# Three late expert weights loaded early, inputs turned two tiles ahead, and a GpSimd product by a broadcast tensor in an attention and mixture-of-experts block

## What is computed

```
mod = (silu(c) @ wmod) in 6 parts: sa, ca, ga, sb, cb, gb        # |ga|, |gb| at least 0.25, sign kept
h = layernorm(x) * (1 + ca) + sa
x = x + ga * attention(h)       # 16 heads of 16, causal softmax, output projection
h = layernorm(x) * (1 + cb) + sb
logits = h @ gate_w             # 8 experts, the 2 largest taken, softmax over the two
y = sum over the two of weight_e * (silu(h @ w1[e]) @ w2[e])     # 256 -> 512 -> 256
x = x + gb * y
```

## Time and profile before

| | |
|---|---|
| median of 3 runs | 1025.18 us (1021.88 to 1030.54) |
| the profiled execution | 1022.33 us, its span 1020.6 us |
| TensorE matmul / VectorE / ScalarE / GpSimd busy | 89% / 71% / 57% / 36% |
| chain that ended last, by engine | PE 60%, DVE 14%, ACT 9%, issue 6%, DMA 4%, POOL 3% |
| Silu of a tile (L1050) | 598 ns mean, 71 of them |
| high part of a tile's inputs (L1044), low part (L1451) | 378 and 424 ns median |
| low part of a tile's hidden values (L1456) | 690 ns mean |
| GpSimd's product with a broadcast tensor (L906) | 747 to 1027 ns, median 750, 9 of them |
| GpSimd's division (L865) | 2361 ns mean |

### The profile page before, as it was taken

How to read it: one execution, slowest core, us unless ns; L and a number is a source line. 1 busy time by engine, 2 the same in 40 slices (tenths; PEclk the granted TensorE clock), 3 DMA queues, 4 the chain that set the end, 5 groups by cost and what they waited for, 6 DMA issues and landing times.

```text
span 1020.6 us, 19387 instructions
## 1 busy us (share of the span) xinstructions
PE 904.9 (89%) x6174; PEld 532.1 (52%) x6174; DVE 727.4 (71%) x2328; ACT 577.6 (57%) x1257; POOL 371.9 (36%) x320
## 2 busy tenths in 40 slices
PE   6899799998899999989999888778799999999990
PEld 3543335433535334544443443322698898999880
DVE  8788766879576889657789677877447574444687
ACT  3345576676576677586676657757434443334452
POOL 1422030251423124324103333074386466565530
PEclk7999999999999999999999999999899999999995
DMA  8456526426406257254365473104423213222789
GB/s 276 125 63 126 76 68 137 76 64 118 71 9 139 56 86 144 76 60 112 53 117 116 110 146 138 35 25 127 136 75 97 94 64 109 74 80 72 219 271 299
DMA packets 83236, 110.62 MB, mean 108 GB/s; under 512 B 15930, under 2 KB 56434, under 8 KB 83138
## 3 DMA queue, kind: packets, MB, share of 16 engines
q1 hardware_dynamic: 75506, 89.45, 38.7%
q0 software_dynamic: 6816, 18.62, 5.8%
q10 hardware_dynamic: 816, 1.32, 0.4%
HBM read 69.42 MB, written 35.41 MB: 103 GB/s over the span
## 4 chain that ended last, share of the span: by engine, by line
PE 60%; DVE 14%; ACT 9%; issue 6%; DMA 4%; POOL 3%; SPq 2%; another core or an unknown queue 1%; POOLq 0%; ACTq 0%; DVEq 0%
PE PO L1612 10%; PE PH L1489 8%; PE PY L1489 8%; PE PS L1592 8%; PE PM L1569 7%; ACT PR L992 3%; PE PHT L1697 2%; PE PX L1624 2%; PE PX L1538 2%; DVE MXF L1295 2%; DVE JK L1292 2%; DMA LD<-OS 2%; PE PS L1596 2%; PE PX L1547 1%; PE PX L1548 1%
## 5 line engine op out<-in xcount | busy, mean ns | idle before, releaser
L992 ACT ACTIVATE PR<-PS 128x512 f32<-128x512 f32 (+3 forms) x768 | 334.5, 497 | 149.9 <-PE PS L1596 113.3
L1292 DVE CUSTOM_DVE_ANT_0 JK<-PM,MK 128x128 bf16<-128x128 f32 (+3 forms) x512 | 239.1, 484 | 54.7 <-PE PM L1569 53.5
L1569 PE MATMUL PM<-QK 128*128 128x512 bf16 (+3 forms) x768 | 247.4, 331 | 24.7 <-DVE MXF L1295 15.2
L1592 PE MATMUL PS<-QK 128*128 128x512 bf16 (+3 forms) x768 | 245.9, 331 | 12.6 <-ACT PR L992 10.4
L1295 DVE TENSOR_REDUCE MXF<-PM 128x1 f32<-128x512 f32 x256 | 175.2, 685 | 76.8 <-PE PM L1569 75.0
L1592 PEld LDWEIGHTS PS<-QK 128*128 128x128 bf16 x768 | 74.9, 98 | 170.3 <-ACT PR L992 105.0
L1612 PE MATMUL PO<-PR,V 128*17 128x512 f32 (+3 forms) x1536 | 162.8, 496 | 0.0
L1569 PEld LDWEIGHTS PM<-QK 128*128 128x128 bf16 x768 | 75.1, 98 | 100.4 <-DVE MXF L1295 37.4
L1489 PE MATMUL PY<-W2S,HT 128*128 x852 | 120.4, 291 | 5.5 <-issue 5.3
L1489 PE MATMUL PH<-W1S,XT 128*128 x426 | 114.0, 403 | 7.9 <-DVE XT L1451 6.9
L1050 ACT ACTIVATE HS<-PH 128x512 f32<-128x512 f32 x71 | 42.5, 598 | 138.4 <-PE PH L1489 115.6
(11 more groups left out here) (263 smaller groups left out, 1210.0 us busy)
## 6 DMA issues: line engine op xcount, KB each, us to landing
QK<-SD SPq DMA_DIRECT2D x180, 128.0 KB
SD<-SP SPq DMA_DIRECT2D x42, 256.0 KB, 2.8
OP<-OS SPq DMA_DIRECT2D x64, 64.0 KB
LP<-LR SPq DMA_DIRECT2D x64, 64.0 KB, 2.3
W1S<-in_w SPq DMA_DIRECT2D x8, 512.0 KB, 7.2
W2S<-in_w SPq DMA_DIRECT2D x8, 512.0 KB, 4.6
X<-XA SPq DMA_DIRECT2D x3, 1024.0 KB, 9.6
H2D<-XA SPq DMA_DIRECT2D x3, 1024.0 KB, 4.9
```

Of the source, the lines that this page charges most:

```text
L992: eng.activation(PR[:, slot, i, c0:512], PS[m % 3][:, c0:512], ACT.Exp, scale=0.25).then_inc(S["exp"].sem, 1)
L1292: eng.tensor_tensor_reduce(JK[:, jk % 2, 0:w], PM[m % 3][:, 0:w], MK[:, 512 - w:512], 1.0, -3.0e38, ALU.add, ALU.max, MXA[:, mb, h, qt:qt ...
L1569: eng.matmul(PM[m % 3][:, 0:128 * (k1 - k0)], QK[:, r, h, 0, qt * 128:(qt + 1) * 128], QK[:, r, h, 1, k0 * 128:k1 * 128], start=True, stop ...
L1592: last = eng.matmul(PS[m % 3][:, c0:512], QK[:, r, h, 1, j * 128:(j + 1) * 128], QK[:, r, h, 0, 512 * f + c0:512 * f + 512], start=True, s ...
```

## The change

Four things. The loads of the second weights of experts 4, 5 and 6 go, as soon as the load of expert 3 has been issued, into other buffers that are free by then: `G3` (modulation rows that are no longer read) for 4 and 5, `XN` for 6; `raw(e)` names the place. `cut` 4 moves from ScalarE to VectorE. Inputs are turned two tiles ahead, gathers are issued five tiles ahead instead of three (there are still three buffers and one PSUM bank), and the cuts and rests stand earlier in the list. And the second GpSimd product in the table multiplies by `PI` as a broadcast tensor instead of by `PI` as a scalar of each partition.

```diff
@@ schedule()
     for e in range(4):
         place(NG - 1, 2 + e, one("wload", 1, e))
+        if e < 3:
+            place(NG - 1, 6 + e, one("wload", 1, 4 + e))
...
-    early = {0: [("cut", 4)], 1: [("cut", 5), ("rest", 5)], 2: [("cut", 6), ("rest", 6), ("cut", 7), ("rest", 7)]}
-    order += [("wload", 1, 4), ("wload", 1, 5), ("od", NG - 1), ("wload", 1, 6), ("wload", 1, 7), ("turnx", 0)]
+    early = {0: [("rest", 5), ("cut", 6)], 1: [("rest", 6), ("cut", 7), ("rest", 7)]}
+    order += [("wload", 1, 7), ("od", NG - 1), ("turnx", 0), ("xload", 3), ("cut", 4), ("turnx", 1), ("xload", 4), ("rest", 4), ("cut", 5)]
     for t in range(NF + 12 + NT):
         now[0] = t
-        if t + 3 < NF:
-            order.append(("xload", t + 3))
         if 0 <= t - 3 < NF:
             order.append(("ystore", t - 3))
         if t < NF:
             order.append(("up", t))
-        if t == 1:
-            order.append(("rest", 4))
-        if t + 1 < NF:
-            order.append(("turnx", t + 1))
+        if t + 2 < NF:
+            order.append(("turnx", t + 2))
+        if t + 5 < NF:
+            order.append(("xload", t + 5))
         if 0 <= t - 1 < NF:
             order.append(("turnh", t - 1))
         order += early.get(t, [])
@@ where the loaded weights lie
+        def raw(e):
+
+            if 4 <= e < 6:
+                return G3R[:, 4 * (e - 4):4 * (e - 3), :]
+            return XN[:, :, :] if e == 6 else W2L[:, e].bitcast(F32)
@@ sync_program, wload 1, e
-                        sp.wait_ge(*after("st", "score", NG - 2 if e < 4 else NG - 1, len(SCORES) - 1, 1))
-                        sp.wait_ge(*after("px", "tok", 0, seg_tiles(0) * 2 // PAIRS[0] - 1))
-                        if e > 5:
+                        if e < 4:
+                            sp.wait_ge(*after("st", "score", NG - 2, len(SCORES) - 1, 1))
+                            sp.wait_ge(*after("px", "tok", 0, seg_tiles(0) * 2 // PAIRS[0] - 1))
+                        elif e < 6:
+                            sp.wait_ge(S[f"h2s{B - 2}"], 16)
+                        elif e == 6:
+                            sp.wait_ge(*after("px", "lg", B - 2, 3))
+                        else:
                             sp.wait_ge(*after("pv", "pv", NG - 1, 1, 7))
@@ gpsimd_program, hot
-                    eng.tensor_scalar(both[:, :, 0, :], high, PI[:, 0:1], None, ALU.mult).then_inc(S["both"].sem, 1)
+                    eng.tensor_tensor(both[:, :, 0, :], high, PI[:, 0:1].unsqueeze(2).broadcast_to([128, np, t1 - t0]),
+                                      ALU.mult).then_inc(S["both"].sem, 1)
@@ scalar_program, out of the last batch into XN
+                        if b == B - 1:
+                            ac.wait_ge(*after("sp_d", "rest", 6))
@@ scalar_program, cut e, now only for e >= 5
                     ac.wait_ge(*after(f"w0{e}", "wload", 1, e))
-                    eng.activation(W2H[:, e], W2L[:, e].bitcast(F32), ACT.Copy).then_inc(S["sp_a"].sem, 1)
+                    ac.wait_ge(*after("st", "score", NG - 1, len(SCORES) - 1, 1))
+                    if e > 5:
+                        ac.wait_ge(*after("pv", "pv", NG - 1, 1, 7))
+                    eng.activation(W2H[:, e], raw(e), ACT.Copy).then_inc(S["sp_a"].sem, 1)
@@ vector_program, cut e, now for e < 5
+                    if e == 4:
+                        dv.wait_ge(*after("st", "score", NG - 1, len(SCORES) - 1, 1))
+                    eng.tensor_copy(W2H[:, e], raw(e)).then_inc(S["sp_d"].sem, 1)
```

More of the change, by code:

```diff
@@ L373 @@
     "split": {"sp_a": 1},
-    "cut": {"sp_d": lambda e: int(e < 4), "sp_a": lambda e: int(e >= 4)},
+    "cut": {"sp_d": lambda e: int(e < 5), "sp_a": lambda e: int(e >= 5)},
     "rest": {"sp_d": 1},
@@ L762, in sync_program @@
                     else:
-                        sp.wait_ge(*after("st", "score", NG - 2 if e < 4 else NG - 1, len(SCORES) - 1, 1))
-                        sp.wait_ge(*after("px", "tok", 0, seg_tiles(0) * 2 // PAIRS[0] - 1))
-                        if e > 5:
+                        if e < 4:
[6 more added lines that the diff above has]
+                        else:
                             sp.wait_ge(*after("pv", "pv", NG - 1, 1, 7))
-                        eng.dma_start(W2L[:, e, :, :].bitcast(F32), w2[e].rearrange("(k p) f -> p k f", p=128)).then_inc(S[f"w0{e}"].sem, 16)
+                        eng.dma_start(raw(e), w2[e].rearrange("(k p) f -> p k f", p=128)).then_inc(S[f"w0{e}"].sem, 16)
                 elif kind == "gat":
@@ L1032, in scalar_program @@
                     eng.activation(W1H[:, e], W1L[:, e].bitcast(F32), ACT.Copy).then_inc(S["sp_a"].sem, 1)
-                elif kind == "cut" and a[0] >= 4:
+                elif kind == "cut" and a[0] >= 5:
                     e = a[0]
                     ac.wait_ge(*after(f"w0{e}", "wload", 1, e))
-                    eng.activation(W2H[:, e], W2L[:, e].bitcast(F32), ACT.Copy).then_inc(S["sp_a"].sem, 1)
+                    ac.wait_ge(*after("st", "score", NG - 1, len(SCORES) - 1, 1))
+                    if e > 5:
+                        ac.wait_ge(*after("pv", "pv", NG - 1, 1, 7))
+                    eng.activation(W2H[:, e], raw(e), ACT.Copy).then_inc(S["sp_a"].sem, 1)
                 elif kind == "turnx":
@@ L1439, in vector_program @@
                     eng.tensor_tensor(W1L[:, e], W1L[:, e].bitcast(F32), W1H[:, e].bitcast(F32), ALU.subtract).then_inc(S["sp_d"].sem, 1)
-                elif kind == "cut" and a[0] < 4:
+                elif kind == "cut" and a[0] < 5:
                     e = a[0]
                     dv.wait_ge(*after(f"w0{e}", "wload", 1, e))
-                    eng.tensor_copy(W2H[:, e], W2L[:, e].bitcast(F32)).then_inc(S["sp_d"].sem, 1)
+                    if e == 4:
+                        dv.wait_ge(*after("st", "score", NG - 1, len(SCORES) - 1, 1))
+                    eng.tensor_copy(W2H[:, e], raw(e)).then_inc(S["sp_d"].sem, 1)
                 elif kind == "rest":
                     e = a[0]
-                    dv.wait_ge(*after("sp_d" if e < 4 else "sp_a", "cut", e))
-                    eng.tensor_tensor(W2L[:, e], W2L[:, e].bitcast(F32), W2H[:, e].bitcast(F32), ALU.subtract).then_inc(S["sp_d"].sem, 1)
+                    dv.wait_ge(*after("sp_d" if e < 5 else "sp_a", "cut", e))
+                    eng.tensor_tensor(W2L[:, e], raw(e), W2H[:, e].bitcast(F32), ALU.subtract).then_inc(S["sp_d"].sem, 1)
                 elif kind == "turnx":
```

## The result

The changed kernel took 1011.14 us (median of 4 runs, 1008.94 to 1020.02) where the kernel before took 1024.53 (4 runs, 1021.88 to 1030.54) on the same chip: a ratio of 0.988, 95% interval 0.984 to 0.992. Measured once more it was 0.990 (0.988 to 0.991; 1009.74 against 1020.10). The profiled execution took 1009.88 us, its span is 1008.1.

A forecast was written before the change was run, and what follows sets the result against it. GpSimd was taken to pace the table, VectorE and TensorE the last attention group, late weight splits the experts' start. 2.5 + 3.0 + 2.5 + 1.3 + 2.0 = 11.3 us off 1022.33, plus 2.85, gave 1013.9; range 1009 to 1022.

The forecast's parts named there:

- The table, 2.5: Routing table, paced by GpSimd: the broadcast product saves 0.37 us in each of seven steps, taken as 2.5 us.
- let the 0.92 fall on the new product just the same: Routing table: VectorE's masks, blamed for 0.92 us of the old product's 2.04, would lengthen the new one by as much.
- one of the signs of being wrong that the prediction named: Routing table: the prediction is wrong if the table follows TensorE or VectorE rather than GpSimd; no size given.
- Rival (b): Routing table: VectorE's hindrance doesn't follow to the new product, saving 5.5 us instead of 2.5, 1010.9 us; chance 0.13.
- (d): Routing table: VectorE's masks hurt the new product far more; at 3.9 us a product, slower than before, 1029.4 us; chance 0.07.
- (e): Routing table: the new product is slightly longer, 2.0 us lost instead of 2.5 won, 1018.4 us; chance 0.05.
- The start, 3.0: Start of the experts: with earlier loads and cuts, the first down product starts 2.75 us earlier, one more turn done, 0.25.
- The clock, 2.5: Behind the first down product: the longest pause falls to some 1.9 us, TensorE's clock holds, 2.5 us saved.
- rival (a): From 712 us: the clock falls all the same because the whole stretch is thin, 2.5 less saved, 1016.4 us; chance 0.20.
- Turning two ahead, 1.3 in the middle: Expert tiles: up products stop waiting for low input halves; the 1.09 at 774.30 and bits of 0.2 and 0.3 go.
- The combining stretch, 2.0: Combining stretch, 955 to 997 us: two-ahead turning saves at most 3.5 and at least 0 with VectorE busy; taken as 2.0.
- Late next: Last batch's softmax reciprocal, behind rest 7: GpSimd's division ends at 734.3, projection needs it at 735.8, 1.5 us to spare.

The follow-up runs named there:

- the small kernel: Separate kernel without the block's computation, timing five scalar and five broadcast GpSimd products beside idle or busy VectorE: at rest 1.12 and 0.75 us.
- number early: Changed kernel with TensorE fetching the first tile's expert number right behind turn 0 instead of before the first up product: 1010.02 us, ratio 0.991.
- without lookahead: Changed kernel with inputs turned one tile ahead and gathers issued three ahead again, the rest of the change kept: 1012.54 us, ratio 0.992.
- the dummies: Changed kernel with the first expert number fetched early and 16 unread matmuls before the first down product, run twice: ratios 0.990 and 0.989.
- product only: Kernel before with the second GpSimd product by a broadcast tensor and nothing else: 1017.18 us against 1020.72, ratio 0.997.
- before again: Kernel before, unchanged, run once more for a second profile: 1020.44 us, span 1018.7.
- after again: Changed kernel, unchanged, timed once more and profiled a second time: 1009.74 us against 1020.10, ratio 0.990.
- the kernel with the second turn behind: Changed kernel turning one tile ahead up to iteration 4, two from there, iteration 4's second turn behind its down product: 1013.92 us, ratio 0.993.

## Why the prediction was right, and where not

1013.9 was forecast and 1011.14 measured; 11.3 us were to be saved. By the columns, second profile against second profile, it is 344.53 - 336.43 = 8.1: table 1.7, start 3.3, to the projection 0.8, from there to the last tile 2.4, group and end -0.2. The timed medians differ by 13.4 the first time and 10.4 the second; 2.3 of the 10.4 the columns don't locate. By parts of the change it is 1.7 for the product, 4.9 for the early loads and cuts (3.5 and 1.4, the latter the clock) and 0.4 for turning two ahead (336.81 - 336.43). So the sign and rough size were right. That the time came within 3 us is in part luck: the forecast stood on a median of 1025.18, and the kernel before had medians of 1020.10 to 1021.48 in the later calls. Each term has its own account.

- **The table, 2.5.** It gave 1.7, and not by "let the 0.92 fall on the new product just the same". The product lost 0.70, not 0.37 (1.34, predicted 1.7). What was left out is that the hindrance works both ways: the masks together grew by 0.82, and in the later steps a loop became the bound: table matmuls (685.02), add (685.52), two masks (685.71 to 687.89), two products (the first from 687.98), and then the matmuls of two steps later, so that a step is half of it. Four steps gained 0.45 each, the last product 0.37, and the first three steps lost 0.5. The time follows VectorE and GpSimd together, one of the signs of being wrong that the prediction named; GpSimd alone had set it before. Rival (b) fell with the 1.34, and (d) and (e) too: 0.75 at rest, 1.96 at most. The Trainium skill ("GPSIMD Engine Reference", the sections on performance versus the Vector engine and on engine selection) has two-input work at about 2.6 cycles an element and one-input work near line rate; the small kernel's 0.75 agrees with the first and its 1.12 contradicts the second.
- **The start, 3.0.** The walk of the queues gave 11.54 us from the first turn's second transposition to the first down product (11.7 from the first); the two profiles have 12.22, with the clock fallen between, and 11.36. Right in size. Its path was not quite right: the walk has no wait of turn 3 for its gathered rows, which is what sets the start in the second profile (number early). Not seen either were the register fetch, which costs nothing while turn 3 waits anyhow, and the price of the lookahead there: 0.5 us.
- **The clock, 2.5.** "I expect it to hold" failed; this is the step of the prediction that was wrong. The pause of 1.9 was forecast to a tenth (1.90 and 1.79), but the comparison with the pause of 1.77 in 960 to 970, behind which the clock stayed at 1.00, didn't carry over: the dummies show that here the clock answers to the pause. The size of the old fall was about right: before, 14.36 and 14.51, without a fall and without lookahead 12.09, so 2.3 and 2.4. The new fall is shorter and costs 1.5 to 1.7 (13.50 to 13.69 against 11.96), so about 0.8 came back. Whether the change gave even that isn't shown: "product only", with the old pause of 4.28, also had the short fall and 13.50. The forecast gave all of the 2.5 back, rival (a) none; (a) is nearer, though for the pause and not for a thin stretch.
- **Turning two ahead, 1.3 in the middle.** The rows it rested on, 1.09 and 1.77, were accidents of one execution; the second profile has neither. Turning two ahead did give 0.64, elsewhere: at tile 10, behind the last batch's layer norm statistics on VectorE.
- **The combining stretch, 2.0.** Measured 1.97; that it fits so well is luck, since 2.0 was picked between bounds of 0 and 3.5 (the kernel without lookahead falls back by 0.64 up to tile 62 and 2.61 at the last, against the dummies' run). The copies of the last tiles show how, before again and after again:

```profile
975.43 0.41 DVE L1463 COPY YO<-PY 128x256 f32<-128x256 f32 x1
...
979.32 0.41 DVE L1463 COPY YO<-PY 128x256 f32<-128x256 f32 x1
...
982.72 0.42 DVE L1463 COPY YO<-PY 128x256 f32<-128x256 f32 x1
```

```profile
971.79 0.42 DVE L1482 COPY YO<-PY 128x256 f32<-128x256 f32 x1
...
975.68 0.42 DVE L1482 COPY YO<-PY 128x256 f32<-128x256 f32 x1
...
978.31 0.42 DVE L1482 COPY YO<-PY 128x256 f32<-128x256 f32 x1
```

  Two of three tiles take 3.90 either way, with VectorE full of the combination; every third one takes 2.63 with two turned ahead and 3.40 with one.
- **Late next.** The division of the attention output was given 1.5 us to spare. In both profiles of the changed kernel it had 0.7. Without lookahead it ended at 737.33, 0.3 before the projection at 737.65, and in the kernel with the second turn behind it did bind.

## What to carry to other kernels

Take a second profile before a wait of one or two microseconds becomes a term of a sum: what the second doesn't have is the execution's own, whatever name the profile gives the releaser. A product moved to a faster form beside VectorE must be costed with what it does to VectorE. Where a walk of the queues is made by hand, the landing of the gathers belongs in it. A pause of TensorE can have a second price, the clock behind it, and work that nobody reads can fill it; and where a distance in a pipeline grows, one iteration has two of everything, so it belongs where no other queue is near its due time.

## What the runs showed of the hardware

- A GpSimd product of 336 bf16 elements a partition takes 1.12 us with a scalar of each partition and 0.75 with a broadcast tensor.
- Beside VectorE comparisons with two SBUF inputs, the broadcast product takes 1.34 and the comparison of 768 elements 1.39 instead of 0.96 (small kernel); copies out of PSUM hinder neither product, and copies within SBUF lengthen them to 1.18 and 0.81.
- After a TensorE pause of 1.8 us the granted clock went to 0.50 in three executions (after, after again, number early), and with 16 matmuls in the pause, leaving 0.48, it stayed at 1.00 twice. It also stayed at 1.00 behind pauses of 0.8 at the same place (four executions), and behind one of 1.77 at another place (960 to 970 in the kernel before), so the length of the pause alone doesn't decide.
- Behind the same pause of 4.28 us the clock was down for about 6.8 us in one execution (before) and 3.4 in another (product only).
